# Order of four stages in a four-layer transformer kernel on one NeuronCore

## The reference

```
x = x + quant_expert(layernorm(x), gu, ctx)        # two linear layers with int8-like rounding
x = x + ternary_ffn(layernorm(x), w1, w2, w3)      # sigmoid(x w1) * (x w2), then w3
x = x + cross_attention(layernorm(x), ctx, Wq, Wk, Wv, Wo)   # 16 heads of 128, 256 context rows
x = x + shared_ffn(layernorm(x)) + comb * routed_ffn(layernorm(x))   # silu-gated, 1024 + 128 wide
```

## Time and profile before

| | |
|---|---|
| median of 3 runs | 396.44 us (396.07 to 398.32) |
| the profiled execution | 396.23 us, of it the span 394.5 |
| granted TensorE clock | 1.000 |
| busy in the span: PE, DVE, ACT, POOL | 382.1, 299.7, 232.1, 164.7 us |
| the chain that ended last | PE 72%, DVE 13%, ACT 4%, issue 3%, POOL 3%, DMA 3% |

### The profile page before, as it was taken

How to read it: one execution, slowest core, us unless ns; L and a number is a source line. 1 busy time by engine, 2 the same in 40 slices (tenths; PEclk the granted TensorE clock), 3 DMA queues, 4 the chain that set the end, 5 groups by cost and what they waited for, 6 DMA issues and landing times.

```text
span 394.5 us, 8400 instructions
## 1 busy us (share of the span) xinstructions
PE 382.1 (97%) x2978; PEld 358.5 (91%) x2978; DVE 299.7 (76%) x975; ACT 232.1 (59%) x616; POOL 164.7 (42%) x263
## 2 busy tenths in 40 slices
PE   7898999999999999999999999999999999999996
PEld 6788898898898999998999999998999899999896
DVE  4787979789866889788766989787757777765644
ACT  1897777775644466666554466766554666664342
POOL 2114676864624344244453345235353243332231
PEclk9999999999999999999999999999999999999999
DMA  7999210000000200000000100000000000000000
GB/s 244 321 348 393 79 32 2 2 2 0 3 2 0 83 4 1 2 1 2 1 28 2 58 1 2 0 2 2 1 28 2 0 2 0 2 0 2 29 2 27
DMA packets 15114, 16.86 MB, mean 43 GB/s; under 512 B 1569, under 2 KB 14049, under 8 KB 15073
## 3 DMA queue, kind: packets, MB, share of 16 engines
q1 hardware_dynamic: 15072, 16.33, 12.8%
HBM read 15.28 MB, written 1.05 MB: 41 GB/s over the span
## 4 chain that ended last, share of the span: by engine, by line
PE 72%; DVE 13%; ACT 4%; issue 3%; POOL 3%; DMA 3%; SPq 1%; DVEq 0%; POOLq 0%
PE bank_qa L396 10%; PE bank_pt L609 6%; PE bank_s L589 6%; PE bank_o L642 6%; PE bank_u L625 5%; PE bank_s L396 5%; PE bank_s L597 3%; PE bank_s L513 3%; PE bank_o L646 3%; PE bank_pt L396 3%; PE bank_u L629 3%; DMA wq_raw<-in_wqT 3%; DVE prob L1638 2%; PE bank_u L724 2%; PE bank_pt L513 2%
## 5 line engine op out<-in xcount | busy, mean ns | idle before, releaser
L1282 POOL TENSOR_SCALAR prob<-prob,row_inv,valid_b 128x256 f32<-128x256 f32 x128 | 70.3, 559 | 79.3 <-DVE row_inv L1646 79.2
L983 ACT ACTIVATE prob<-prob,row_min 128x256 f32<-128x256 f32 x128 | 64.2, 502 | 54.2 <-DVE row_min L1638 54.1
L1651 DVE TENSOR_TENSOR pt_lo<-bank_pt,pt_hi 128x512 fp32r<-128x512 f32 x64 | 43.9, 685 | 16.3 <-ACT pt_hi L936 16.3
L1638 DVE CUSTOM_DVE_ANT_0 prob<-bank_s,masked 128x256 f32<-128x256 f32 x128 | 48.8, 419 | 3.5 <-PE bank_s L597 2.4
L1293 POOL TENSOR_TENSOR act_lo<-act_raw,act_hi 128x256 fp32r<-128x256 f32 x32 | 24.2, 756 | 45.2 <-ACT act_hi L1048 45.0
L609 PE MATMUL bank_pt<-ident,prob 128*128 128x128 f32 x256 | 40.5, 276 | 1.2 <-POOL prob L1282 0.8
L936 ACT ACTIVATE pt_hi<-bank_pt 128x512 fp32r<-128x512 f32 x64 | 37.5, 587 | 4.6 <-PE bank_pt L609 4.3
L396 PE MATMUL bank_qa<-xt_hi,a_hi 128*128 128x256 f32 x126 | 39.6, 314 | 0.3 <-DVE qa_lo L1619 0.3
L609 PEld LDWEIGHTS bank_pt<-ident,prob 128*128 128x128 f32 x256 | 29.6, 141 | 7.5 <-POOL prob L1282 2.2
L396 PE MATMUL bank_qa<-xt_lo,a_hi 128*128 128x256 f32 x126 | 35.5, 282 | 0.0
L396 PE MATMUL bank_qa<-xt_hi,a_lo 128*128 128x256 f32 x126 | 35.5, 282 | 0.0
(11 more groups left out here) (326 smaller groups left out, 1201.1 us busy)
## 6 DMA issues: line engine op xcount, KB each, us to landing
wq_raw<-in_wqT SPq DMA_DIRECT2D x4, 512.0 KB, 8.2
wo_raw<-in_wo SPq DMA_DIRECT2D x4, 512.0 KB, 8.3
w_raw<-in_w12T SPq DMA_DIRECT2D x2, 704.0 KB, 7.3
gate_raw<-in_gateT SPq DMA_DIRECT2D x2, 576.0 KB, 7.6
up_raw<-in_upT SPq DMA_DIRECT2D x2, 576.0 KB, 9.9
down_raw<-in_downT SPq DMA_DIRECT2D x2, 576.0 KB, 12.3
x<-in_x SPq DMA_DIRECT2D x4, 256.0 KB, 6.7
guT<-in_guT SPq DMA_DIRECT2D x4, 256.0 KB, 3.5
```

The source lines that it names most:

```text
L983: act.activation(row, row, ACT.Exp, scale=-1.0, bias=row_min[:, h % 2, t:t + 1], accum_out=row_sum[:, h % 2, t:t + 1]).then_inc(S["s_exp"], 1)
L1282: pool.tensor_scalar(row, row, row_inv[:, h % 2, t:t + 1], valid_b[:, 0:1], ALU.mult, ALU.mult).then_inc(S["s_norm"], 1)
L1638: dve.tensor_tensor_reduce(out=prob[:, h % 2, t, :], in0=src[:, t * T:(t + 1) * T], in1=masked[:, :], scale=1.0, scalar=3.0e38, op0=ALU.ad ...
L1651: dve.tensor_tensor(pt_lo[:, :, cols], bank["pt"][:, :].rearrange("p (s t) -> p s t", s=2), f32(pt_hi[:, :, cols]), ALU.subtract).then_inc ...
```

## The change

There are five edits to the order, under four headings in the change's own words.

- Scores ahead of queries: in `attention` the two calls change places, in all four batches.
- Rounding behind scaling: POOL does all of the first part's rounding at head 4, behind the scaling of head 5's probabilities, rather than half of it at head 3.
- The second layer's first part (of the quantised expert) one head sooner: the activation's turn goes from (8, 0) to (7, 1), the spread from (9, 1) to (8, 1), DVE's ratio from head 8 to 7, POOL's root from head 9 to 8, the scaling of the rows from head 10 to 9; maxima, scales and rounding stay at 10. In batch 0 the statistics go from head 9 to 11 and their power on POOL from 11 to 13.
- Before the last batch's last layer, `ffn_begin` goes ahead of the last late chunk's `ffn_down`.
- The last chunk of the last batch writes its up half to bank qa and its gate half to its own bank; the sigmoid waits for the gate half alone, and DVE's second product waits for the rest.

```diff
+        def gate_alone(b, p):
+            return b == NB - 1 and p == FFN_CHUNKS - 1
+
+        def up_half(b, p):
+            return bank["qa"][:, T:2 * T] if gate_alone(b, p) else ffn_bank(b, p)[:, T:2 * T]
...
                     turn_probs(b, h)
+                    if h + 2 < H:
+                        scores(b, h + 2)
                     if h + 4 < H:
                         queries(b, h + 4)
-                    if h + 2 < H:
-                        scores(b, h + 2)
...
-                        last = split_mm(dst[:, at:at + T], w_hi[:, k, cols], w_lo[:, k, cols], yt_hi[:, k, :],
-                                        yt_lo[:, k, :], first, k == ND - 1)
+                        half = dst[:, 0:T] if at == 0 else up_half(b, p)
+                        last = split_mm(half, w_hi[:, k, cols], w_lo[:, k, cols], yt_hi[:, k, :], yt_lo[:, k, :],
+                                        first or (gate_alone(b, p) and k == 0), k == ND - 1)
                         first = False
+                    if at == 0 and gate_alone(b, p):
+                        last.then_inc(S["ffn_gate"], 1)
...
-            Q_STEPS = {(0, 1): 0, (5, 0): 1, (5, 1): 2, (8, 0): 3, (9, 1): 4, (11, 1): 5, (12, 0): 6}
+            Q_STEPS = {(0, 1): 0, (5, 0): 1, (5, 1): 2, (7, 1): 3, (8, 1): 4, (11, 1): 5, (12, 0): 6}
...
                     ffn_down(b - 1, FFN_CHUNKS - 2)
+                    ffn_begin(b, last)
                     ffn_down(b - 1, FFN_CHUNKS - 1)
-                    ffn_begin(b, last)
...
             def ffn_sig(b, p):
-                act.wait_ge(S["ffn_mm"], FFN_CHUNKS * b + p + 1)
+                if gate_alone(b, p):
+                    act.wait_ge(S["ffn_gate"], 1)
+                else:
+                    act.wait_ge(S["ffn_mm"], FFN_CHUNKS * b + p + 1)
...
-                    if not last and h == 9:
+                    if not last and h == 8:
                         q_root1(b + 1)
...
-                    if h == 3:
+                    if h == 4:
                         q_round(b + 1, 0, 0)
-                    if h == 4:
                         q_round(b + 1, 0, 1)
...
-                    if b == 0 and h == 11:
+                    if b == 0 and h == 13:
                         lnq_power(2, NB)
...
+                if gate_alone(b, p):
+                    dve.wait_ge(S["ffn_mm"], FFN_CHUNKS * (b + 1))
...
-                    elif h == 8:
+                    elif h == 7:
                         q_ratio1(nxt)
-                    elif h == 9 and b == 0:
+                    elif h == 9:
+                        q_scaled_w(nxt, 1)
+                        q_scaled_x(nxt, 1)
+                    elif h == 10:
+                        q_rowmax(nxt, 1, slice(0, 4))
+                        q_scales(nxt, 1)
+                    elif h == 11 and b == 0:
                         dve.wait_ge(S["x_in"], 16 * (NB - 2))
                         link(lnq_stats_of([2, 3]))
                         lnq_variances([2, 3])
-                    elif h == 10:
-                        q_scaled_w(nxt, 1)
-                        q_scaled_x(nxt, 1)
-                        q_rowmax(nxt, 1, slice(0, 4))
-                        q_scales(nxt, 1)
```

More of the change, by code:

```diff
@@ L271, in build @@
                     att_x route_mm route_copy route_t route_d route_sig route_w
-                    ffn_mm ffn_sig ffn_prod ffn_hi ffn_lo ffn_lo_last ffn_y shared_x routed_x ffn_x""".split():
+                    ffn_gate ffn_mm ffn_sig ffn_prod ffn_hi ffn_lo ffn_lo_last ffn_y shared_x routed_x ffn_x""".split():
             S[n] = sem(n)
@@ L1682, in ffn_act @@
                                               op0=ALU.add, op1=ALU.mult))
-                dve.scalar_tensor_tensor(out=act_raw[:, r, :], in0=sig[:, r, :], scalar=0.5, in1=src[:, T:2 * T],
+                if gate_alone(b, p):
+                    dve.wait_ge(S["ffn_mm"], FFN_CHUNKS * (b + 1))
+                dve.scalar_tensor_tensor(out=act_raw[:, r, :], in0=sig[:, r, :], scalar=0.5, in1=up_half(b, p),
                                          op0=ALU.mult, op1=ALU.mult).then_inc(S["ffn_prod"], 1)
```

## The result

| | before | after |
|---|---|---|
| median | 396.38 us (396.07 to 398.32, 4 runs) | 390.94 us (390.23 to 392.61, 4 runs) |
| ratio to before | | 0.9863, 95% interval 0.984 to 0.9887 |
| profiled execution, of it the span | 396.23, 394.5 us | 390.37, 388.6 us |

The forecast was 392.3. The kernel is 1.4 us faster than that, just outside the forecast's own range (391.3 to 393.6) and inside the stated one (390.9 to 395.2), by 0.04 us only, which is luck in a kernel whose four runs spread over 2.4. Of 35 runs of before beside the first experiments, 25 had a mean granted clock of 0.998 to 1.000 and a median of 396.78 us, and 10 had one of 0.993 to 0.996 and a median of 398.48.

The account below looks back on a forecast made before the run. TensorE, busy 382.1 of 394.5 us, was taken as the bound, its late starts as the loss. Terms 1.07 + 1.42 + 0.64 + 0.62 + 0.33 = 4.08 us gave 392.3 us; own range 391.3 to 393.6, stated range 390.9 to 395.2.

Parts of the forecast that it names:

- 1. Scores ahead of queries: Heads 0 to 2 of the batches: waits around scores and queries shrink, 1.07 us, bounds 0.3 and 1.5; steady heads 0.
- 2. Rounding behind scaling: Head 5 of batches 0 to 2: transposes no longer wait for POOL's scaling, 0.60 + 0.41 + 0.41 = 1.42 us.
- The turn of the rounded rows: Head 5, TensorE: four roundings in a row leave 0 to 0.1 us of cover; lower bound 0.3 less in all.
- 3. The second layer's part: Heads 9 and 12: 0.94 us gained in batches 1 and 2, batch 0 -0.30; sum 0.64, bounds -0.6 and 1.9.
- The second pair at head 9: Head 9's second pair of transposes is 0.18 late behind POOL's scaling, 0.24 with the restart.
- the wait at head 13: Batch 0: a new wait of about 0.55 at head 13, giving back part of the removed waits.
- The loss at the norm: Batch 0: DVE's norm runs beside POOL's scaling; -0.30 taken for batch 0, loss 0.4 by the skill's rule.
- 4. First chunk ahead: Batch 3's last layer: second chunk starts at 371.61 rather than 372.23, 0.62 us; bounds 0.2 and 0.7.
- 5. Gate half: Last chunk of batch 3: DVE's product starts at about 388.77 rather than 389.10, 0.33 us; bounds 0 and 0.41.
- the tail: Both edits of batch 3's last layer, the first chunk and the gate half: 0.95 us together.
- A: Rival: removed waits come back as others on DVE and POOL; 2.0 us left, 394.4; chance 0.22.
- C: Rival: slower; odd heads' later queries delay exponentials, TensorE waits in each pair, costing 7.2 us, 399.5; chance 0.05.
- D: Rival: batch 0 follows the matmuls after all (+0.8), gate half brings 0.1 more; 391.4; chance 0.09.

Follow-up runs that it names:

- the first experiments: Four kernels, each the kernel before with one part of the change alone (scores, rounding, third edit, both tail edits): 395.22, 395.23, 395.37 and 395.52 us.
- e3: Kernel before with only the whole third edit: second layer part's steps a head sooner, batch 0's statistics at head 11; 395.37 us, ratio 0.9960.
- e7: Changed kernel with POOL's power and DVE's statistics for batches 2 and 3 moved from batch 0 to batch 1's second layer; 391.32 us, ratio 0.9848.
- e8: Changed kernel with DVE's inverses of head 1 of batch 3 put ahead of batch 2's shared residual; 391.82 us, ratio 0.9862.
- e9: Changed kernel with batch 2's shared residual on DVE put behind head 0's low half and head 2's row minima in the last batch; 391.01 us, 0.9848.

## Why the prediction was right, step by step

The forecast (faster, all waits but batch 0's gone) is the case that came. Against its sum of 4.08 the traces have 5.27 and 5.10.

**1. Scores ahead of queries: mis-sized, 1.07 against 1.53 to 1.57,** just over the upper bound. The mechanism held in batch 3, 0.57 against 0.51 to 0.59. The step that failed is the part put at nothing without a sum, "the minima are held by DVE's low half of the probabilities anyway ... so I take 0". Ten minima in heads 0, 1, 5, 6 and 10 were held by the scores, 2.4 us of DVE's idle time, and outside heads 0 to 2 the edit brings 0.30 in the whole (by which of them isn't shown). At heads 0 to 2 the terms were 0.16 short in sum. The idle sum was one row of the groups of instructions, and I had read only timelines.

**2. Rounding behind scaling: right.** 1.42 forecast, 1.52 at the three places (0.64, 0.44, 0.44). The turn of the rounded rows, which I gave 0 to 0.1 us of cover, brought no wait that shows.

**3. The second layer's part: right in kind, 0.64 against 1.07.** Batches 1 and 2: 0.52 and 0.55 against 0.47 each. The second pair at head 9 was 0.05 late and not 0.24, since amax started 0.09 sooner than I said (0.42 behind the turn against 0.51), and head 9's transposes came 0.07 later behind the turn (3.01 against 2.94). At head 12 the pace was misread by 0.13: 182.98 less the lateness of 0.36 is 182.62, not 182.75; the scaling was ahead of either. Batch 0: I had -0.30, and alone it is 0.01 (in the whole, -1.17 less the 0.57 to 0.61 of edit 2 and the 0.47 of edit 1, it leaves 0.1 gained). Its chain did what I said: the wait at head 13 behind the low half (0.26; I had 0.55), 0.12 at the mix, 0.20 at head 14's second pair. Head 14, which I had no sooner, came 0.19 sooner in e3, and 0.06 of that was left at head 15. The loss at the norm did not come, and there I had misread the trace: I said the norm would come to lie beside POOL's scaling. It lay there already. Before:

```profile
106.33 1.25 POOL L1282 TENSOR_SCALAR prob<-prob,row_inv,valid_b 128x256 f32<-128x256 f32 x2
106.82 0.90 DVE L1418 TENSOR_SCALAR hs<-x,ln_mv,ln_rstd 128x256 f32<-128x256 f32 x2
```

So 0.90 is to be compared with 0.98 after, and the price was 0.1. By the rule of the Trainium skill (SBUF — State Buffer, SBUF: two separate sides) on the port pair that DVE and GpSimd share, the first step would wait for POOL's row to end and 0.4 be lost. It didn't: after, DVE's first step starts 0.30 into POOL's first row and lasts 0.41, as alone. Nor is it shown that the rule applies. Its condition, as the prediction has it, is a two-port mode of DVE, and 0.41 is as long as DVE takes for a product of two inputs of this size (0.42).

**4. First chunk ahead: right.** 0.62 forecast; the second chunk starts at 366.81 against 372.23, 5.42 sooner, of which 4.78 was there at head 15: 0.64. The first chunk started 0.65 behind ACT's start, as said.

**5. Gate half: right.** 0.33 forecast, 0.34 to 0.39 measured.

The forecasts of edits 1, 2, 3 and the tail fall short by 0.46, 0.10, 0.43 and 0.13 (with 1.53, 1.52, 1.07 and 1.08 measured): 1.12 of the 1.19 us between 4.08 and 5.27. The 0.59 ahead of head 0 in the profiled execution are no part of the change; they are TensorE's shorter wait for ACT's copies of the weights. Of the rivals, A (waits come back as others) is what happens to e7, e8 and e9, not to the change; C's place, a wait in each odd head, is empty: between heads 4 and 11 of batch 3 the distances are those of before within 0.02 us. D gave the right time (391.4) for part of the reason: batch 0 did not lose, but it did not follow the matmuls either.

## What to carry to other kernels

When one engine is 97% busy, count the lateness of its starts against its own undisturbed pace, and price each removal by that; this gave three of five terms within 0.1 us. Before a wait's removal is put at nothing in the places not looked at, read the idle sum of the instruction that waits, over the whole run: it names the places to look at, though not what they are worth (here six of ten waits brought nothing). And when a wait's releaser is moved, look at the next two on the same engine: twice here the name changed and most of the lateness stayed. Compare executions at the same granted clock, and traces from a point behind the first loads: 1.4 us between two kernels were the clock alone.

## What the runs showed of the hardware that I had not expected

DVE's norm step (128x256, tensor_scalar) lasts 0.40 to 0.41 us alone. It lasts 0.90 where POOL's subtraction (tensor_tensor, 0.73) starts 0.02 behind it, once in before and once in after. Where the same subtraction starts 0.14 to 0.27 behind it, six times in before, it lasts 0.40 to 0.41 again, and at 0.14 and 0.15 POOL's subtraction takes 0.85. Here one such pair in before, two steps and the subtraction beside the second:

```profile
125.18 0.74 DVE L1418 TENSOR_SCALAR hs<-x,ln_mv,ln_rstd 128x256 f32<-128x256 f32 x2
125.66 0.85 POOL L1293 TENSOR_TENSOR act_lo<-act_raw,act_hi 128x256 fp32r<-128x256 f32 x1 [0.51 <-ACT act_hi L1048]
```

Beside POOL's scaling (tensor_scalar, rows of 0.55) the first step lasts 0.40 to 0.42 and the second 0.57 to 0.66, and POOL's second row 0.60 to 0.72. So who loses, and how much, depends on when each starts, and not only on what POOL runs; a rule for it can't be drawn from these few pairs.

The attention repeats within 0.1 us per batch from execution to execution. The first 58 us vary by 2.6 us, and 1.0 to 1.1 of that comes from 3.4 us of TensorE at 1.2 GHz, in three traces of 14.
